# Layer 1's router logits in two halves around the first shared gate-up, with VectorE's shared products moved up among its routing operations

## What is computed

```python
x = x + _L0_ffn_ref(_L0_cond_ref(x, itok_B_0_7, L0_cond_weights), ...)      # 8 experts, top 2, capacity
x = x + _L1_ffn_ref(_L1_cond_ref(x, ...LoRA weights..., itok_B_0_7), ...)   # 16 experts, top 4, and a shared one
```

```python
logits = h @ router_w.T                       # 1024 x 16
probs = softmax(logits); top_vals, top_idx = top_k(probs, 4)
top_vals = top_vals / maximum(top_vals.sum(-1), 1e-9)
routed = sum over the 4 chosen experts of silu(h w_gate[e]) * (h w_up[e]) @ w_down[e], weighted
shared = silu(h @ sh_gate) * (h @ sh_up) @ sh_down    # 704 hidden values
out = routed + sigmoid(h @ sh_gate_w) * shared
```

## Time and profile before

| | us |
|---|---|
| median of 3 runs (lowest and highest) | 419.85 (419.69 and 419.85) |
| the profiled execution, its own time | 418.48 |
| its span in the trace | 416.7 |
| TensorE busy, matmuls | 399.2 (96% of the span) |
| VectorE busy | 226.4 (54%) |
| ScalarE busy | 148.1 (36%) |
| GpSimd busy | 165.7 (40%) |

### The profile page before, as it was taken

One profiled execution on the slowest core, in us unless ns is written; L12 is line 12 of the kernel. 1 busy time (PEld: TensorE's weight loads), 2 busy tenths in 40 slices (PEclk: granted clock), 3 DMA queues, 4 the chain that ended last, 5 costly groups with the idle time before them and its releaser, 6 DMA issues.

```text
span 416.7 us, 6135 instructions
## 1 busy us (share of the span) xinstructions
PE 399.2 (96%) x1931; PEld 325.2 (78%) x1931; DVE 226.4 (54%) x514; ACT 148.1 (36%) x349; POOL 165.7 (40%) x153
## 2 busy tenths in 40 slices
PE   1999999999989999999999999999999999999995
PEld 1877888888768888888887878888888888888784
DVE  6965545454595312112116797576555556555467
ACT  1544343434344333233334452344232222322140
POOL 2600223112133332443331212775777777743400
PEclk9989999999999999999999899999999999999999
DMA  7501622444271233331010126862333334311194
GB/s 226 197 6 50 175 92 88 132 133 134 62 261 52 87 114 127 127 126 39 12 30 35 39 101 158 180 208 76 103 102 105 107 107 100 104 67 61 65 361 142
DMA packets 17207, 46.78 MB, mean 112 GB/s; under 512 B 3466, under 2 KB 6050, under 8 KB 16874
## 3 DMA queue, kind: packets, MB, share of 16 engines
q1 hardware_dynamic: 12666, 34.07, 25.8%
q0 software_dynamic: 4512, 12.33, 9.8%
HBM read 38.10 MB, written 8.29 MB: 111 GB/s over the span
## 4 chain that ended last, share of the span: by engine, by line
PE 85%; DVE 10%; ACT 2%; issue 1%; DMA 1%; SPq 0%; DVEq 0%; ACTq 0%
PE gu L1152 13%; PE gu L1154 13%; PE gu L1153 13%; PE y L1436 10%; PE gu L1419 7%; PE y L1152 5%; PE y L1154 5%; PE y L1153 5%; PE gu L1428 2%; PE gu L1371 2%; PE gu L1416 2%; PE gu L1421 2%; PE gu L1417 2%; DVE act_f L1113 2%; PE gu L1178 2%; PE gu L1351 1%
## 5 line engine op out<-in xcount | busy, mean ns | idle before, releaser
L464 POOL TENSOR_TENSOR w_lo<-w_raw,w_hi 128x512 fp32r<-128x512 f32 (+3 forms) x44 | 52.9, 1221 | 154.0 <-ACT w_hi L525 139.6
L1152 PE MATMUL gu<-act_hi,w_hi 128*128 128x512 f32 x196 | 79.7, 407 | 0.7 <-DVE hid L789 0.7
L1154 PE MATMUL gu<-act_hi,w_lo 128*128 128x512 f32 x196 | 78.3, 400 | 0.0
L1153 PE MATMUL gu<-act_lo,w_hi 128*128 128x512 f32 x196 | 78.0, 398 | 0.0
L549 ACT ACTIVATE hid_hi<-hid 128x512 fp32r<-128x512 f32 x46 | 29.0, 633 | 89.7 <-DVE hid L789 48.2
L499 POOL DMA_INDIRECT y_k<-w_raw,put x47 | 46.2, 983 | 27.8 <-DVE w_raw L1071 19.5
L789 DVE TENSOR_TENSOR hid<-silu,gu 128x512 f32<-128x512 f32 x24 | 16.5, 687 | 67.6 <-PE gu L1154 67.5
L1436 PE MATMUL y<-w_dn,t_hidT 88*128 x188 | 48.3, 380 | 0.6 <-DVE t_hidT L1078 0.6
L802 DVE TENSOR_TENSOR hid_lo<-hid,hid_hi 128x512 fp32r<-128x512 f32 x46 | 31.7, 692 | 27.6 <-ACT hid_hi L549 26.7
L1152 PEld LDWEIGHTS gu<-act_hi,w_hi 128*128 128x128 f32 x196 | 37.7, 192 | 9.7 <-DVE hid L789 1.2
L1154 PEld LDWEIGHTS gu<-act_hi,w_lo 128*128 128x128 f32 x196 | 37.5, 192 | 9.0
(11 more groups left out here) (226 smaller groups left out, 699.0 us busy)
## 6 DMA issues: line engine op xcount, KB each, us to landing
w_raw<-in_wc SPq DMA_DIRECT2D x8, 576.0 KB, 3.8
w_raw<-in_w SPq DMA_DIRECT2D x11, 384.0 KB, 3.2
w_raw<-in_w_gu SPq DMA_DIRECT2D x8, 352.0 KB, 4.2
w_gu<-in_w_gu SPq DMA_DIRECT2D x8, 352.0 KB, 4.6
w_gu<-y_k SPq DMA_DIRECT2D x5, 512.0 KB, 6.4
w_raw<-scr SPq DMA_DIRECT2D x8, 256.0 KB, 4.4
w_dn<-in_w_dn SPq DMA_DIRECT2D x1, 1936.0 KB
w_raw<-in_ws SPq DMA_DIRECT2D x5, 384.0 KB, 3.2
```

The source lines that it names most:

```text
L464: nc.gpsimd.tensor_tensor(w_lo[par][:, w], w_raw[par][:, w], w_hi[par][:, w].bitcast(F32), ALU.subtract).then_inc(split, 1)
L1152: T.matmul(out, w[0], x[0], start=start, stop=False)
L1153: T.matmul(out, w[0], x[1], start=False, stop=False)
L1154: return T.matmul(out, w[1], x[0], start=False, stop=stop)
```

## The change

TensorE computes the router logits of blocks 0 to 3, then gate-up (0,0), then the logits of blocks 4 to 7; the semaphore for VectorE is raised behind the second half alone. On VectorE product (0,0) goes ahead of the wait for the logits, hid_low (0,0) between the maxima and their indices, product (0,1) ahead of the wait for the ranks, hid_low (0,1) one place up, and product (1,0) between `slot_rows(0)` and `slot_values(0)`. No instruction is added or removed except waits: the wait for the routers' weights stands twice.

```diff
--- before.py
+++ after.py
@@ -924,16 +924,17 @@
             def down_low(k):
                 weights_low(k, dn_cols(SH), s_whd, s_w)
 
+            shared_prod(0, 0)
             dve.wait_ge(s_logit, 2)
             chain(V.tensor_copy(r_logit[:], logit1_ps.rearrange("p (t e) -> p t e", t=NT)))
             for t in range(NT):
                 ins = V.max(r_top[:, t, :], r_logit[:, t, 0:E1])
             chain(ins)
+            shared_low(0, 0)
             for t in range(NT):
                 ins = V.max_index(r_idx[:, t, :], r_top[:, t, :], r_logit[:, t, 0:E1])
             chain(ins)
             chain(V.tensor_copy(r_idf[:], r_idx[:]))
-            shared_prod(0, 0)
             dim = [P, K1, NT, E1]
             chain(V.tensor_tensor(r_oh[:], cst0[:, CI_IOTA:CI_IOTA + E1].unsqueeze(1).unsqueeze(1).broadcast_to(dim),
                                   r_idf[:, :, 0:K1].rearrange("p t k -> p k t").unsqueeze(3).broadcast_to(dim), ALU.is_equal))
@@ -944,7 +945,7 @@
             V.tensor_scalar(r_lg[:, :, E1], r_logit[:, :, E1], -1.0, None, ALU.mult)
             V.tensor_tensor(r_lg[:, :, E1 + 1:], r_top[:, :, 0:K1], peak.broadcast_to([P, NT, K1]),
                             ALU.subtract).then_inc(s_rlg, 1)
-            shared_low(0, 0)
+            shared_prod(0, 1)
 
             dve.wait_ge(s_rank, 2)
             dim = [P, E1, NT]
@@ -958,11 +959,10 @@
             chain(V.tensor_scalar(first[:], ahead[:], float(P), -1.0, ALU.mult, ALU.add))
             chain(V.tensor_tensor(slot[:], rank1_ps.rearrange("p (t e) -> p t e", t=NT),
                                   first[:].unsqueeze(1).broadcast_to([P, NT, E1]), ALU.add))
-            shared_prod(0, 1)
+            shared_low(0, 1)
             chain(V.tensor_tensor(r_kept[:].rearrange("p k t e -> p k (t e)"), r_oh[:].rearrange("p k t e -> p k (t e)"),
                                   slot[:].rearrange("p t e -> p (t e)").unsqueeze(1).broadcast_to([P, K1, NT * E1]),
                                   ALU.mult))
-            shared_low(0, 1)
             chain(V.reduce_sum(slot_k[:], r_kept[:], axis=AX_X))
             chain(V.tensor_copy(slot_i[:], slot_k[:]))
             shift_by = P.bit_length() - 1
@@ -986,8 +986,8 @@
             dve.wait_ge(s_ct, 3)
             dve.wait_ge(s_x2t, 4)
             slot_rows(0)
+            shared_prod(1, 0)
             slot_values(0)
-            shared_prod(1, 0)
             slot_rows(1)
             shared_low(1, 0)
             slot_values(1)
@@ -1169,15 +1169,16 @@
                                         wblk[:, t].rearrange("p b d -> p (b d)"), start=True, stop=True)
                 last.then_inc(s_xc, 1)
 
-            def logits(ps, done, off, ne):
+            def logits(ps, done, off, ne, first=0, last_t=NT):
                 pe.wait_ge(s_in["routers"], 16)
-                for t in range(NT):
+                for t in range(first, last_t):
                     if t % 4 == 0:
                         pe.wait_ge(s_actf, done + (t // 4 + 1) * KH)
                     for k in range(KH):
                         last = T.matmul(ps[:, t * ne:(t + 1) * ne], act_f[:, k, t * P:(t + 1) * P],
                                         routers[:, off + k * ne:off + (k + 1) * ne], start=k == 0, stop=k == KH - 1)
-                last.then_inc(s_logit, 1)
+                if last_t == NT:
+                    last.then_inc(s_logit, 1)
 
             eye = cst[:, CS_ID:CS_ID + P]
 
@@ -1378,9 +1379,10 @@
             def shared_dn(k, s):
                 down(SH, c + k, (c + k) % 2, s, start=k == 0, stop=k == NA - 1)
 
-            logits(logit1_ps, 2 * KH, SM_R1, LOGIT1)
+            logits(logit1_ps, 2 * KH, SM_R1, LOGIT1, 0, NT // 2)
             pe.wait_ge(s_actl, 5 * KH)
             shared_gu(0, 0)
+            logits(logit1_ps, 2 * KH, SM_R1, LOGIT1, NT // 2, NT)
             turn_x2(0)
             pe.wait_ge(s_actl, 6 * KH)
             shared_gu(0, 1)
```

## The result

The changed kernel takes 421.89 us (median of 22 runs), the kernel before 420.11 in as many; the ratio is 1.0038, with a 95% interval of 1.0022 to 1.0055. On 419.85 us that is 1.6 us more (0.9 to 2.3). The forecast was 1.07 us more. One run of the kernel before took 1027 us and counts as slow; the ratio leaves it out. The profiled execution has a span of 418.3 us, before 416.7. All in front of the change lies 0.10 us earlier in this trace than in the one before, so distances between the two traces need that much added.

A forecast was written before the change was run, and what follows sets the result against it. TensorE was taken as the bound, with 85% of the chain that ended last, VectorE's routing deciding in the changed stretch. 3.11 us of delay less 2.04 gave plus 1.07: 419.85 to 420.9 us, range 420.1 to 422.5.

The forecast's parts named there:

- The clock: TensorE's gate-up (0,0): with the logits halved it keeps 2.4 GHz and ends at 232.30, putting TensorE 1.69 us ahead.
- TensorE's new wait: TensorE before the ranks: stands still from 237.23 to 239.3 for multi, about 2.0 us, giving back the clock's gain.
- VectorE's first part: VectorE up to the one-hots: about 0.5 us wait for ScalarE's hid_hi; multi ready at 239.26, before at 237.90.
- The wait that decides: VectorE's product (0,1) waits for silu (0,1) behind Exp and table load; r_thr at 242.56, 3.11 us later.
- From r_thr to product (1,0): VectorE's stretch between these two: moved operations take 2.04 us out, 8.61 before and 6.57 now.
- The floor by TensorE's own path: TensorE via the copy of block 1: up half of (1,1) no earlier than 249.08, plus 0.29 us.
- The rule on the table load: ScalarE before silu (0,1): the skill page's extra drain, about 1.38 us, would make the total plus 2.5 us; trace preferred.
- rival D: ScalarE between table load and silu (0,1): a 1.28 us drain makes product (1,0) 1.3 us later, 422.2 us; chance 0.02.
- A: Rival at silu (0,1): ready by 239.8, so the clock's gain reaches the end, 418.8 us; chance 0.10.
- B: Rival, no change: the chain is shorter than summed and TensorE's floor holds, plus 0.3 to 0.8 us; chance 0.17.
- C: Rival, slower through TensorE's half clock, in gate-up (0,0) (422.6 us) or in the stall before the ranks; chance 0.11.
- C's second case: Half clock comes in TensorE's 2.0 us stall before the ranks, slowing some 12 matmuls behind it: 421.9 to 422.1 us.

The follow-up runs named there:

- e5: Changed kernel with ScalarE's Exp behind the copy of turned block 3 and TensorE's ranks behind turn 1 and down (0,0); ratio 0.9948 to the kernel before.
- e3: Changed kernel with product (0,1) and hid_low (0,1) back at their old places behind slot and r_kept; ratio 0.9996 to the kernel before.
- e4: Changed kernel with ScalarE's Exp, and with it both table loads, moved behind the copy of turned block 3; ratio 0.9982 to the kernel before.
- r8: Repeat of e8, the changed kernel with Exp, ranks and GpSimd's low part of chunk 2 all later; ratio 0.9962 to the kernel before, slots 1.70 us earlier.
- e2: Kernel before with VectorE's half of the change alone, all router matmuls ahead of gate-up (0,0); ratio 1.0078 to the kernel before, slots 3.42 us later.
- r2: Repeat of e2, VectorE's half of the change alone on the kernel before; ratio 1.0110 to the kernel before, slots 4.93 us later.
- e8: Changed kernel with three more moves: Exp, TensorE's ranks and GpSimd's low part of chunk 2 later; ratio 0.9962 to the kernel before, slots 1.70 us earlier.
- r6: Changed kernel with GpSimd's low part of weight chunk 2 also waiting for VectorE's gate values; ratio 1.0011 to the kernel before, slots 0.78 us later.
- e7: Kernel before with all 32 router matmuls behind gate-up (0,0) in one stretch; ratio 1.0026 to the kernel before, slots 2.80 us later.

## Why the prediction was right, point by point

- *The clock.* Right: 1.00 through gate-up (0,0), and 1.00 behind the gap of 2.1 us. That the halves would keep it was taken, not worked out; the nine traces bear it out. The gate-up's matmuls end at 232.26 (231.87 + 0.39), forecast 232.30.
- *TensorE's new wait.* Forecast 2.0 us before the ranks, measured 2.14, with multi as its releaser. That the gain of the clock is given back there is right; that this gap costs nothing by itself, e5 shows.
- *VectorE's first part.* The wait for hid_hi, forecast 0.5, is 0.63; multi starts at 238.99, forecast 238.97 (0.12 late with the 0.10 in front).
- *The wait that decides.* Product (0,1) at 242.04 and r_thr at 242.65, forecast 241.95 and 242.56. With the 0.10 by which this trace is ahead, 0.19 later than my sum. e3 and e4 show that this wait is the cause: each takes it away in its own way and loses all or more of the 1.75 us.
- *From r_thr to product (1,0): the term that was mis-sized.* I put 6.57 us (8.61 less 2.04), and it took 7.06 (242.65 to 249.71). `upto` took 0.95 more beside GpSimd's operation; against that, slot_i, which had been the one beside it in the trace before (0.56 us), came down to 0.18 us, 0.38 less. That is 0.57. The other 0.08 goes off because I counted the row one-hots at their length, 1.22, where product (1,0) starts 1.14 behind their start (248.57 to 249.71). I had taken each operation's duration from a row of its own without asking what GpSimd did at that moment, and had moved the operations without moving that. 0.19 and 0.49 added to 1.07 give the 1.75. The 0.68 that is missing is more than the 0.4 us that I gave the forecast as its own uncertainty: the path was right, its price was not.
- *The floor by TensorE's own path.* I put plus 0.29 as long as silu (0,1) is late. e3, where this path is last, ends at plus 0.10: the right path, 0.2 too dear. In the change itself its gate half ends at 249.62, not 249.08, since down (0,1) waits for hid_low (0,1), which comes behind the long `upto`.
- *The rule on the table load.* The Trainium skill, "ScalarE: Activation LUTs", section "What ACT_TABLE_LOAD costs", has a drain of about 1.38 us in a switch. After the change as before, the silu starts 0.01 us behind the load (240.05 + 1.28 = 241.33, 241.34). The measurement decides: rival D is out.
- *The other rivals.* A (silu (0,1) ready in time) is what e4 and r8 make true, and they show the gain that it stood for: 0.7 and 1.7 us. B and C did not come; in the change no clock fell behind the gap. C's second case was not empty, though: in e2 and r2 the clock does fall behind a gap of this length, against the rows that I had put against it.

The interval of the measured loss, 0.9 to 2.3 us, holds the forecast of 1.07 and the traces' 1.75, so the whole times alone could not have told the two apart; the traces do.

## What to carry to other kernels

Before an operation is moved up on one engine, look at what its input stands behind on the engine that makes it: here a silu behind an Exp and a table load, so that a product moved 'into idle time' held the chain up for 2.4 us. A gain on one engine counts at the point where it meets the chain that is last; here 1.69 us of clock turned into a 2.1 us gap. The way to use the clock's gain is to take away what stands in the chain that is last, piece by piece (e4, e8). And where two engines hold each other up when they run at the same time, a move shifts the meeting as well as the operation.

## What the runs showed of the hardware that I had not expected

A small VectorE operation can wait out a whole GpSimd operation. `upto`, 0.17 us by itself, took 1.12 and ended 0.02 us behind GpSimd's; in e4 it was hid_lo, 1.72 instead of 0.69; with GpSimd elsewhere (r6, r8) both are at their own lengths, 0.17 and 0.69. Not every operation is held up: in e3 slot_k's reduction ran at its usual 0.68 us inside GpSimd's operation, and the conversion slot_i behind it waited for the end. VectorE and GpSimd in e3:

```profile
246.98 0.68 DVE L966 TENSOR_REDUCE slot_k<-r_kept 128x32 f32<-128x512 f32 x1
247.69 0.57 DVE L967 CAST slot_i<-slot_k 128x32 int32<-128x32 f32 x1
```

```profile
246.88 1.35 POOL L464 TENSOR_TENSOR w_lo<-w_raw,w_hi 128x512 fp32r<-128x512 f32 x1 [11.95 <-ACT w_hi L525]
```

The Trainium skill, "SBUF — State Buffer", section "Terms", describes VectorE and GpSimd arbitrating for a shared port pair that one of them holds for a whole instruction. The ends agree with it: `upto` ends 0.02 us behind GpSimd's operation, slot_i in e3 0.03 behind, and hid_lo in e4 0.54 behind, most of its own length of 0.69. That the port is the cause no run here shows; what is shown is that the two operations hold each other up (r6, r8).

TensorE's clock went to half speed with the engine at work without a pause, on 32 matmuls of 18 columns (3.5 us), in whichever place they stood (before, e2, r2, e7), and kept 1.00 with the same 32 in two lots around 12 wide ones, in all nine traces. Layer 0's 32 router matmuls of 8 columns, which stand in one stretch in every kernel here, have a half clock behind or in them in all thirteen traces. Behind an idle gap of 2.1 us the clock stayed at 1.00 in five traces (the change, e3, e4, e6, r6) and fell in e2 and r2. Where in or behind the narrow stretch it falls differs from run to run, and so does how long it stays down: in e2 it fell some 0.8 us into the gate-up for 3.4 us, in r2 inside the narrow stretch for 6.8 us, which cost 1.5 us more (the two ran on different chips).
